# A graph network on one core: the store of the count rows issued by ScalarE instead of by SyncE

## The chip, the cores and the metric

The kernel runs on one core of one Trainium2 chip. The metric is the device time of one execution in microseconds (us), the median of several runs. The engines are TensorE (PE in the profile; PEld is its weight load), VectorE (DVE), ScalarE (ACT), GpSimd (POOL) and SyncE (SP). A row with "SPq" or "ACTq" is a transfer issued by that engine; the time in it is how long the engine stood at the issuing instruction, not how long the data took.

## The reference

The inputs are 6250 nodes of 128 features and 206250 edges, sorted by destination, with a weight each. Four layers are added to x one after the other, each on `h = relu(layernorm(x))`:

```python
x = x + segment_sum(w[:, None] * (sigmoid(h @ Wg + bg) * (h @ W))[dst], src)   # L0
x = x + segment_sum(h[src], dst) @ W1.T + b1                                   # L1
x = x + layer 2: messages from h[src] and h[dst] summed at dst, then a linear update
x = x + layer 3: hypergraph convolution, batch norm over all nodes, relu
```

All four need sums over the same edges. The kernel makes them dense: a matrix of edge counts between nodes, and for L0 the matrix of edge weights.

## The kernel before

The nodes lie in 49 tiles of 128 (`TILES`). After a preparation of about 240 us comes the *build*, one pass over the 49 tiles `j`. It makes for each tile 128 rows of three matrices, each 128 x 6272 numbers in fp16: the counts, and the weights as a high and a low part. It also carries L0 along. Then four phases (`ph` 1 to 4) multiply the stored counts with the node features.

In the build a tile is made in 8 steps `h` of 2 units `u`, 16 units in all:

- VectorE (`hots`, lines 788 to 791) writes one-hot tiles `hot_c` and `hot_r`, two buffers deep. It also adds finished sums to X (`add_four`, line 803), 13 a tile.
- TensorE (`half_windows`, lines 531 to 533) multiplies them into PSUM, 12 matmuls a unit. `take_high` (line 514) subtracts the high part again, so that the low part is left. `sums` (lines 506 to 508) multiplies the turned weights of tile j - 2, `wt`, with the gated features, `g_in`. This is L0, and it waits for both transposing transfers of tile j - 2 before its first product, in step h = 0.
- ScalarE (`build`, line 1033) copies counts and high parts of each unit from PSUM to `stage`, and in `low_parts` (line 1016) the low part two units later. `stage[:, b]` has three slabs (0 counts, 1 high, 2 low) and two buffers, `b` = j mod 2. Before it writes the first unit of tile j, ScalarE waits for what tile j - 2 still needs of the same buffer: `stored{b}` and `wt_in{b}`.
- SyncE (`hand_on`) issues the transfers of a tile. The whole queue is in program order.

The body of `hand_on` before the change, with a = 0 for the high and a = 1 for the low part:

```python
sp.wait_ge(s(done), (j + 1) * HALVES)             # hi_done, then lo_done
sp.dma_start(g_in[:, b, part], ...)               # L333
sp.dma_start_transpose(wt[:, b, a], stage[...])   # L334, slab 1 + a
...
sp.dma_start(by_source...[:, :, cols], stage[:, b, 0])   # L336, the store of the counts
```

So for each tile the queue of SyncE holds: g_in and the transposing transfer of the high part, the same of the low part, and last the store of the counts, 1568 KB into the DRAM matrix `by_source` (counts_by_source in the profile), in runs of 256 bytes. Before them SyncE waits (line 332) until the sums of tile j - 2 are done. After tile 0 a second store (line 339, `filled`) writes a column block of padding.

The stores must have landed before phase 1: `counts_stored` is waited for by SyncE, ScalarE and VectorE. The tiles 0 to 6 are written out one by one, the others run in a loop over six tiles at a time.

Of the kernel before, what the change touches and what calls it, by code (L numbers as in the profile page):

```python
# [19 lines left out]
P = 128  # L20
NODES, EDGES = 6250, 206250
TILES = -(-NODES // P)
# [27 lines left out]
HALVES = 2 * TILE_HOTS  # L50
# [73 lines left out]
def gnn_kernel(nc, x, src, dst, edge_weight, w0, wg0, bg0, w1, b1, wm, bm, wu, bu, hyper, w3, b3, gamma, beta, out):  # L124
    ctx = ExitStack()
    with ctx:
# [159 lines left out]
        @block.sync  # L286
        def _(sp):

            for a, b in ((dst, dst_pad), (src, src_pad), (edge_weight.bitcast(I32), w_pad)):
                sp.dma_start(b[0:EDGES].rearrange("(a b) -> a b", a=15), a.rearrange("(a b) -> a b", a=15)).then_inc(s("pad_in"), 16)  # L290
            sp.wait_ge(s("pads"), 2)
            for k, b in ((1, dst_pad), (0, src_pad), (0, w_pad)):
                sp.dma_start(vec(b[EDGES:PADDED]), pad_rows[0:1, k, :]).then_inc(s("pad_in"), 16)

            sp.dma_start(X[:, 0:TILES - 1, :], x[0:(TILES - 1) * P].rearrange("(i p) f -> p i f", p=P)).then_inc(s("x_in"), 16)
            sp.wait_ge(s("x_zero"), 1)
            sp.dma_start(X[0:LAST, TILES - 1, :], x[(TILES - 1) * P:NODES]).then_inc(s("x_in"), 16)

            for to, of in ((w0g[:, 0:P], w0), (w0g[:, P:P + 1], wg0), (w3s[:], w3), (w_h[:, 0], wu[0:P]),
                           (wraw[:, 0], w1), (wraw[:, 1], wm[0:P]), (wraw[:, 2], wm[P:2 * P]), (wraw[:, 3], wu[P:2 * P]),  # L300
                           (b1s[:], spread(b1, P)), (bus[:], spread(bu, P)), (cols[:, 4:5], spread(bg0, 1)),
                           (cols[:, 0:1], bm.rearrange("(a b) -> a b", b=1)), (cols[:, 1:2], b3.rearrange("(a b) -> a b", b=1)),
                           (cols[:, 2:3], gamma.rearrange("(a b) -> a b", b=1)), (cols[:, 3:4], beta.rearrange("(a b) -> a b", b=1))):
                sp.dma_start(to, of).then_inc(s("weights_in"), 16)
            sp.wait_ge(s("x_zero"), 2)
            sp.dma_start(hrows[0:TILES - 1, :], hyper[0:(TILES - 1) * P].rearrange("(i p) -> i p", p=P)).then_inc(s("weights_in"), 16)
            sp.dma_start(hrows[TILES - 1:TILES, 0:LAST], vec(hyper[(TILES - 1) * P:NODES])).then_inc(s("weights_in"), 16)

            sp.wait_ge(s("pad_in"), 96)
            sp.dma_start(dst_run[:], bass.AP(dst_pad.tensor, 0, [[RUN, P], [1, RUN + 1]])).then_inc(s("dst_in"), 16)  # L310
            sp.dma_start(w_run[:], bass.AP(w_pad.tensor, 0, [[RUN, P], [1, RUN]])).then_inc(s("w_in"), 16)
            for k, b in enumerate((src_pad, dst_pad, w_pad)):
                sp.dma_start(table[:, k * P:(k + 1) * P], bass.AP(b.tensor, 0, [[ALIGN, ROWS], [1, P]])).then_inc(s("table_in"), 16)  # L313

            def layers(general):
                if general:
                    for ph in range(5):
                        general_sum(ph)
                    return

                sp.wait_ge(s("g_parts"), SET)
                sp.dma_start(g_dram.rearrange("i p n -> p i n"), G[:].rearrange("p i a f -> p i (a f)")).then_inc(s("g_stored"), 16)
                sp.wait_ge(s("g_stored"), 16)

                def hand_on(j, k, c):

                    b = c % 2
                    if later(j, 2):
                        sp.wait_ge(s("four_done"), (j - 1) * FOURS)
                    for a, done in enumerate(("hi_done", "lo_done")):  # L330
                        part = slice(a * P, (a + 1) * P)
                        sp.wait_ge(s(done), (j + 1) * HALVES)
                        sp.dma_start(g_in[:, b, part], slab(g_dram, j)[:, part]).then_inc(s(f"g_loaded{b}"), 16)  # L333
                        sp.dma_start_transpose(wt[:, b, a], stage[:, b, 1 + a].rearrange("p i d -> p (i d)")).then_inc(s(f"wt_in{b}"), 16)  # L334
                    cols = slice(j * P, (j + 1) * P) if isinstance(j, int) else bass.ds(j * P, P)
                    sp.dma_start(by_source.rearrange("i p n -> p i n")[:, :, cols], stage[:, b, 0]).then_inc(s(f"stored{b}"), 16)  # L336
                    if isinstance(j, int) and j == 0:

                        sp.dma_start(by_source.rearrange("i p n -> p i n")[:, :, TILES * P:], stage[:, b, 0]).then_inc(s("filled"), 16)

                tiles_loop(sp, hand_on, 0)
                counts_stored(sp)
                sp.wait_ge(s("added"), FOURS * TILES)

                for ph in (1, 2, 3, 4):

                    def step(j, k, c, ph=ph):
                        if not on(j):
                            return
                        if ph == 4:  # L350
                            if later(j, SLOTS):

                                sp.wait_ge(s("sum_done4"), j - (SLOTS - 1))
                            else:
                                sp.wait_ge(s("sum_done3"), min(TILES, 46 + c // 2 * 2))
                            sp.dma_start_transpose(a_turned[:, c % SLOTS], slab(by_source, j)[:, 0:TILES * P]).then_inc(s(f"turned_in{c % SLOTS}"), 16)  # L356
                        elif c % 2 == 0:
                            if later(j, SLOTS):

                                sp.wait_ge(s(f"sum_done{ph}"), j - (SLOTS - 2))  # L360
                            elif ph > 1:
                                sp.wait_ge(s(f"sum_done{ph - 1}"), min(TILES, 46 + c))
                            q = pair_at(ph, c) % 3
                            rows = by_source.rearrange("i p n -> p i n")
                            cols = slice(j * P, (j + 2) * P) if isinstance(j, int) else bass.ds(j * P, 2 * P)
                            sp.dma_start(a_pairs[:, q].rearrange("p i a d -> p i (a d)"), rows[:, :, cols]).then_inc(s(f"a_in{q}"), 16)

                    tiles_loop(sp, step, 0)

            def general_sum(ph):  # L370

                sp.wait_ge(s("g_rows_all"), ph + 1)
                sp.dma_start(h_dram.rearrange("(i p) f -> p i f", p=P), rows_all[:]).then_inc(s("g_table"), 16)
                with sp.Fori(0, CHUNKS) as c:
                    sp.wait_ge(s("g_free"), c + (ph * (CHUNKS + 1) + 1))
                    for a, b in enumerate((src_pad, dst_pad, w_pad)):
                        sp.dma_start(edge_in[:, a:a + 1], b[bass.ds(c * P, P)].rearrange("(a b) -> a b", b=1)).then_inc(s("g_in"), 16)

            branch(sp, layers)

            for g in range(6):
                sp.wait_ge(s("x_out"), 8 * (g + 1))
                sp.dma_start(out[g * 8 * P:(g + 1) * 8 * P].rearrange("(i p) f -> p i f", p=P), X[:, g * 8:(g + 1) * 8, :]).then_inc(s("out_stored"), 16)
            sp.wait_ge(s("x_out"), TILES)
            sp.dma_start(out[(TILES - 1) * P:NODES], X[0:LAST, TILES - 1, :]).then_inc(s("out_stored"), 16)
            sp.wait_ge(s("out_stored"), 16 * 7)
# [595 lines left out]
        def _(act):  # L982
# [29 lines left out]
            def layers(general):  # L1012
# [5 lines left out]
                def build(j, k, c):  # L1018
                    b, n = c % 2, k * (SLOTS // 2) + c // 2
                    for u in range(HALVES):  # L1020
                        if later(j, 1) or u >= 2:
                            act.wait_ge(s("low_left"), j * HALVES + (u - 1))
                            low_parts(*before_at(b, c, u))
                        if u == 0 and later(j, 2):

                            act.wait_ge(s(f"stored{b}"), n * 16)
                            act.wait_ge(s(f"wt_in{b}"), n * 32)
                            if isinstance(j, int) and j == 2:
                                act.wait_ge(s("filled"), 16)
                        act.wait_ge(s("unit_done"), j * HALVES + (u + 1))  # L1030
                        bank = 2 * unit_at(c, u)
                        of = ps[:, bank:bank + 2, 0:HALF * WCOLS].rearrange("p k (i x) -> p k i x", i=TILES)
                        a.copy(stage[:, b, 0:2, :, u * SET_COLS:(u + 1) * SET_COLS], of).then_inc(s("hi_done"), 1)  # L1033

                if not general:
                    act.wait_ge(s("g_stored"), 16)
# [94 lines left out]
```

## Time and profile before

| what | value |
|---|---|
| median of 3 runs | 2862.77 us (2861.38 to 2884.23) |
| the profiled execution | 2846.73 us |
| its span on the core | 2844.9 us, mean granted clock 0.954 |
| first and last transposing transfer of the build issued | 244.9 and 1493.6 us |
| mean moved by DMA, whole span | 212 GB/s |

The span is the time from the first to the last instruction on the core. The profiled execution is one run; the median is of other runs. In the rows below, a row of a timeline gives the start in us, the duration in us, engine, line, operation, and in brackets the idle time before it and what ended that.

### The profile page before, as it was taken

To read this page: it belongs to the slowest core of one execution; us is meant where nothing else is said; L and a number is where in the kernel's file an instruction comes from. 1 tells how busy PE (TensorE), PEld (TensorE's weight loads), DVE (VectorE), ACT (ScalarE), POOL (GpSimd) and SP (SyncE) were. 2 spreads that over 40 slices of the span, in tenths; PEclk is the share of its full clock that TensorE was granted. 3 is DMA by queue.
4 is the path that set the end of the run, shared out by engine and by line. 5 is a ranking of instruction groups with operands and counts; after the bars stand their busy time and mean duration, and the time that the engine had idled before them with its cause. 6 is when DMAs were issued, how large, how long until landed. Compare 5 with 4: busy or idle time off the path is not lost.

```text
span 2844.9 us, 72345 instructions
## 1 busy us (share of the span) xinstructions
PE 2373.2 (83%) x27975; PEld 2024.3 (71%) x27975; DVE 1614.5 (57%) x3456; ACT 1214.5 (43%) x2626; POOL 66.4 (2%) x59
## 2 busy tenths in 40 slices
PE   1626898888888888898893999869997799999996
PEld 0414777777776777777772888758886688888884
DVE  5387998898898988898985111232223222212114
ACT  0605777776776777776773000141112211111113
POOL 0430000000000000000000000000000000000000
PEclk9999999999999999999996999979999899999997
DMA  9615999999999999999997999959999699999995
GB/s 280 181 45 114 195 198 196 193 186 195 188 189 188 196 178 200 181 203 193 183 204 185 264 278 274 280 150 251 258 250 257 167 289 291 283 240 252 252 252 121
DMA packets 1784416, 603.26 MB, mean 212 GB/s; under 512 B 1258086, under 2 KB 1781098, under 8 KB 1784093
## 3 DMA queue, kind: packets, MB, share of 16 engines
q1 hardware_dynamic: 1782538, 594.63, 97.8%
q0 software_dynamic: 1600, 4.92, 0.6%
q8 instruction: 176, 2.88, 0.4%
q14 instruction: 102, 0.84, 0.1%
HBM read 276.78 MB, written 109.03 MB: 136 GB/s over the span
## 4 chain that ended last, share of the span: by engine, by line
PE 43%; SPq 21%; DVE 10%; DMA 9%; issue 9%; ACT 6%; DVEq 1%; POOL 1%; ACTq 0%; POOLq 0%
PE ps L578 30%; SPq L334 10%; SPq L356 9%; DMA counts_by_source<-stage 7%; DVE X L803 4%; PE ps L506 3%; PE ps L508 2%; PE ps L507 2%; ACT hbig L992 2%; DMA edge_table<-w_pad 2%; DVE hot_c L791 2%; ACT stage L1033 2%; ACT stage L1016 1%; PE ps L531 1%; SPq L313 1%
## 5 line engine op out<-in xcount | busy, mean ns | idle before, releaser
L578 PE MATMUL ps<-Ha,a_pairs 128*128 128x258 f16 x7203 | 827.0, 275 | 103.6 <-ACT Ha L1061 103.6
L578 PEld LDWEIGHTS ps<-Ha,a_pairs 128*128 128x128 f16 x7203 | 705.3, 98 | 214.8 <-ACT Ha L1061 104.3
L1033 ACT CAST stage<-ps 128x784 f16<-128x784 f32 x784 | 653.5, 834 | 221.3 <-DMA counts_by_source<-stage 98.8
L531 PE MATMUL ps<-hot_c,hot_r 128*128 128x98 f16 x3136 | 517.1, 214 | 11.6 <-DVE hot_c L791 7.4
L532 PE MATMUL ps<-hot_c,hot_r 128*128 128x98 f16 x3136 | 511.7, 213 | 0.0
L533 PE MATMUL ps<-hot_c,hot_r 128*128 128x98 f16 x3136 | 510.7, 213 | 0.0
L1016 ACT CAST stage<-ps 128x392 f16<-128x392 f32 x784 | 396.5, 506 | 208.0 <-PE ps L514 207.9
L506 PE MATMUL ps<-g_in,wt 128*128 128x128 f16 x2401 | 438.5, 225 | 45.4 <-DVE X L803 32.6
L1072 ACT COPY extra<-ps 128x2 f32 (+1 forms) x196 | 31.4, 160 | 1037.9 <-PE ps L578 1037.9
L507 PE MATMUL ps<-g_in,wt 128*128 128x128 f16 x2401 | 435.0, 224 | 0.0
L508 PE MATMUL ps<-g_in,wt 128*128 128x128 f16 x2401 | 434.0, 223 | 0.0
L803 DVE SCALAR_TENSOR_TENSOR X<-ps,X 128x512 f32<-128x512 f32 (+1 forms) x637 | 394.0, 659 | 16.8 <-PE ps L508 15.6
L791 DVE TENSOR_TENSOR hot_c<-hot_c,meta_w 128x1568 f16<-128x1568 f16 x392 | 382.4, 976 | 0.0
L531 PEld LDWEIGHTS ps<-hot_c,hot_r 128*128 128x128 f16 x3136 | 311.5, 99 | 86.7 <-ACT stage L1016 41.8
L514 PE MATMUL ps<-stage,minus 128*128 128x392 f16 x784 | 265.6, 339 | 125.6 <-ACT stage L1033 72.1
L532 PEld LDWEIGHTS ps<-hot_c,hot_r 128*128 128x128 f16 x3136 | 314.1, 100 | 20.7 <-issue 1.6
L533 PEld LDWEIGHTS ps<-hot_c,hot_r 128*128 128x128 f16 x3136 | 314.0, 100 | 0.0
L506 PEld LDWEIGHTS ps<-g_in,wt 128*128 128x128 f16 x2401 | 240.4, 100 | 84.9 <-DVE X L803 74.0
L788 DVE TENSOR_TENSOR hot_c<-iota_c,meta 128x784 f16<-128x784 f16 x392 | 221.9, 566 | 135.7 <-PE ps L533 109.1
L578 PE MATMUL ps<-Hb,a_turned 128*128 128x258 f16 x2401 | 278.0, 274 | 18.7 <-DMA a_turned<-counts_by_source 15.6
L901 DVE TENSOR_TENSOR agg<-ps,low 128x128 f32<-128x128 f32 x98 | 28.6, 292 | 433.4 <-ACT low L1075 433.4
L578 PEld LDWEIGHTS ps<-Hb,a_turned 128*128 128x128 f16 x2401 | 231.9, 98 | 59.6 <-DMA a_turned<-counts_by_source 15.7
(176 smaller groups left out, 2083.3 us busy)
## 6 DMA issues: line engine op xcount, KB each, us to landing
a_pairs<-counts_by_source SPq DMA_DIRECT2D x75, 3136.0 KB, 14.0
counts_by_source<-stage SPq DMA_DIRECT2D x50, 1568.0 KB, 9.6
edge_table<-src_pad SPq DMA_DIRECT2D x1, 6464.0 KB, 27.9
edge_table<-dst_pad SPq DMA_DIRECT2D x1, 6464.0 KB, 49.5
edge_table<-w_pad SPq DMA_DIRECT2D x1, 6464.0 KB, 48.0
gated_parts<-G SPq DMA_DIRECT2D x1, 3136.0 KB, 12.6
g_in<-gated_parts SPq DMA_DIRECT2D x98, 32.0 KB, 3.3
out_x<-X SPq DMA_DIRECT2D x6, 512.0 KB
```

Of the source, the lines that this page charges most:

```text
L334: sp.dma_start_transpose(wt[:, b, a], stage[:, b, 1 + a].rearrange("p i d -> p (i d)")).then_inc(s(f"wt_in{b}"), 16)
L506: mm(o, wt[:, b, 0, i], g_in[:, b, 0:P], start=i % 4 == 0, stop=False, skip_group_check=True)
L507: mm(o, wt[:, b, 0, i], g_in[:, b, P:2 * P], start=False, stop=False, skip_group_check=True)
L508: last = mm(o, wt[:, b, 1, i], g_in[:, b, 0:P], start=False, stop=True, skip_group_check=True)
L531: mm(into(0), rows_, codes(0), start=v == 0, stop=True, skip_group_check=True)
L532: mm(into(1), rows_, codes(1), start=v == 0, stop=False, skip_group_check=True)
L533: last = mm(into(1), rows_, codes(2), start=False, stop=True, skip_group_check=True)
L578: last = mm(ps[:, c % 2, 0:PARTS], a_slot(ph, c, i), moving[:, i], start=i == 0, stop=i == TILES - 1)
L791: v.tensor_tensor(hot_c[:, b, :, 1:1 + WEIGHTS], hot_c[:, b, :, 0].unsqueeze(2).to_broadcast([P, PAIRS, WEIGHTS, WCOLS, 2]), meta_w[:, pai ...
L803: v.scalar_tensor_tensor(xs, ps[:, 6 + e, 0:(hi - lo) * P], 1.0 / (W_UP * H_UP), xs, ALU.mult, ALU.add).then_inc(s("added"), 1)
L1016: a.copy(stage[:, b, 2, :, u * SET_COLS:(u + 1) * SET_COLS], of).then_inc(s("lo_done"), 1)
L1033: a.copy(stage[:, b, 0:2, :, u * SET_COLS:(u + 1) * SET_COLS], of).then_inc(s("hi_done"), 1)
```

## The change

The store of the counts and the padding store leave SyncE's queue. ScalarE issues them after the copy of the last unit of tile j, once all 16 copies of that tile are complete. Semaphores, sources, destinations and sizes are the same. The lines behind the removed ones move up by 5; line 1033 (the copy of counts and high parts) is line 1028 in the changed kernel, and line 1016 (the low part) is line 1011.

```diff
@@ hand_on, SyncE @@
                         sp.dma_start_transpose(wt[:, b, a], stage[:, b, 1 + a].rearrange("p i d -> p (i d)")).then_inc(s(f"wt_in{b}"), 16)
-                    cols = slice(j * P, (j + 1) * P) if isinstance(j, int) else bass.ds(j * P, P)
-                    sp.dma_start(by_source.rearrange("i p n -> p i n")[:, :, cols], stage[:, b, 0]).then_inc(s(f"stored{b}"), 16)
-                    if isinstance(j, int) and j == 0:
-
-                        sp.dma_start(by_source.rearrange("i p n -> p i n")[:, :, TILES * P:], stage[:, b, 0]).then_inc(s("filled"), 16)
@@ build, ScalarE @@
                         a.copy(stage[:, b, 0:2, :, u * SET_COLS:(u + 1) * SET_COLS], of).then_inc(s("hi_done"), 1)
+                    store_counts(j, b)
+
+                def store_counts(j, b):
+
+                    act.wait_ge(s("hi_done"), (j + 1) * HALVES)
+                    cols = slice(j * P, (j + 1) * P) if isinstance(j, int) else bass.ds(j * P, P)
+                    a.dma_start(by_source.rearrange("i p n -> p i n")[:, :, cols], stage[:, b, 0]).then_inc(s(f"stored{b}"), 16)
+                    if isinstance(j, int) and j == 0:
+
+                        a.dma_start(by_source.rearrange("i p n -> p i n")[:, :, TILES * P:], stage[:, b, 0]).then_inc(s("filled"), 16)
```

On SyncE, the written-out tiles 0 and 1 of the build, before (L336 and L339 are the two kinds of store):

```order
L333 DMA g_in<-gated_parts 128x128
L334 DMA_TRANSPOSE wt<-stage 128x49x128
L333 DMA g_in<-gated_parts 128x128
L334 DMA_TRANSPOSE wt<-stage 128x49x128
L336 DMA counts_by_source<-stage 128x49x128
L339 DMA counts_by_source<-stage 128x49x128
L333 DMA g_in<-gated_parts 128x128
L334 DMA_TRANSPOSE wt<-stage 128x49x128
L333 DMA g_in<-gated_parts 128x128
L334 DMA_TRANSPOSE wt<-stage 128x49x128
L336 DMA counts_by_source<-stage 128x49x128
```

and the same two tiles now:

```order
L333 DMA g_in<-gated_parts 128x128
L334 DMA_TRANSPOSE wt<-stage 128x49x128
L333 DMA g_in<-gated_parts 128x128
L334 DMA_TRANSPOSE wt<-stage 128x49x128
L333 DMA g_in<-gated_parts 128x128
L334 DMA_TRANSPOSE wt<-stage 128x49x128
L333 DMA g_in<-gated_parts 128x128
L334 DMA_TRANSPOSE wt<-stage 128x49x128
```

Only the two pairs of a tile are left on SyncE; nothing stands between the second transposing transfer of a tile and the first g_in of the next.

On ScalarE, the border between tile 0 and tile 1, before (the copies of counts and high parts and of low parts alternate without a break):

```order
L1016 CAST stage<-ps 128x49x8
L1033 CAST stage<-ps 128x98x8
L1016 CAST stage<-ps 128x49x8
L1033 CAST stage<-ps 128x98x8
L1016 CAST stage<-ps 128x49x8
```

and now:

```order
L1011 CAST stage<-ps 128x49x8
L1028 CAST stage<-ps 128x98x8
L1035 DMA counts_by_source<-stage 128x49x128
L1038 DMA counts_by_source<-stage 128x49x128
L1011 CAST stage<-ps 128x49x8
L1028 CAST stage<-ps 128x98x8
```

The store stands behind the last copy of counts and high parts of its tile (L1028), and ahead of the low parts (L1011) of that tile's last two units. The padding store comes in tile 0 only.

## Rows read from the trace of the kernel before

**Rows 1.** The page: busy engines, the SP queue, the largest transfers
```profile
PE 2373.2 (83%) x27975; PEld 2024.3 (71%) x27975; DVE 1614.5 (57%) x3456; ACT 1214.5 (43%) x2626; POOL 66.4 (2%) x59
...
DMA  9615999999999999999997999959999699999995
...
q1 hardware_dynamic: 1782538, 594.63, 97.8%
```

**Rows 2.** Waits: engine, line waited for; us in total, times, longest
```profile
ACT stage L1033 <- DMA counts_by_source<-stage: 98.8, 23, 15.7
...
PEld ps L506 <- DMA wt<-stage: 9.9, 2, 8.6
```

**Rows 3.** Timeline of SyncE's queue, two tiles of the build
```profile
351.47 0.33 SPq L333 DMA_DIRECT2D g_in<-gated_parts  x1
351.84 8.71 SPq L334 DMA_TRANSPOSE wt<-stage  x1
360.60 0.58 SPq L333 DMA_DIRECT2D g_in<-gated_parts  x1
361.22 7.64 SPq L334 DMA_TRANSPOSE wt<-stage  x1
368.91 0.58 SPq L336 DMA_DIRECT2D counts_by_source<-stage  x1
374.56 1.78 SPq L333 DMA_DIRECT2D g_in<-gated_parts  x1
...
401.81 0.33 SPq L333 DMA_DIRECT2D g_in<-gated_parts  x1
```

**Rows 4.** Timeline of ScalarE at a border of two tiles
```profile
374.30 0.57 ACT L1016 CAST stage<-ps 128x392 f16<-128x392 f32 x1
378.28 0.81 ACT L1033 CAST stage<-ps 128x784 f16<-128x784 f32 x1 [3.41 <-DMA counts_by_source<-stage]
378.99 0.49 ACT L1016 CAST stage<-ps 128x392 f16<-128x392 f32 x1
```

**Rows 5.** Timeline of VectorE, the same border
```profile
381.67 0.57 DVE L788 TENSOR_TENSOR hot_c<-iota_c,meta 128x784 f16<-128x784 f16 x1 [2.61 <-PE ps L533]
```

**Rows 6.** Timeline of SyncE's queue: first g_in of tile 2 and of the last tile
```profile
300.64 0.33 SPq L333 DMA_DIRECT2D g_in<-gated_parts  x1
...
1484.45 0.35 SPq L333 DMA_DIRECT2D g_in<-gated_parts  x1
```

**Rows 7.** The page, transfers: issues, KB each, median us from issue to landing
```profile
counts_by_source<-stage SPq DMA_DIRECT2D x50, 1568.0 KB, 9.6
...
wt<-stage SPq DMA_TRANSPOSE x98, 11.0
```

**Rows 8.** Lines 334 and 336: ns at the issuing instruction, min/median/max
```profile
L334 SPq DMA_TRANSPOSE wt<-stage x98: 7337/7922/8987, 244.9 to 1493.6; - x98
...
L336 SPq DMA_DIRECT2D counts_by_source<-stage x49: 439/447/1097, 261.1 to 1501.2; - x49
```

**Rows 9.** Timeline of SyncE's queue, the two stores after tile 0
```profile
261.14 0.59 SPq L336 DMA_DIRECT2D counts_by_source<-stage  x1
261.77 7.16 SPq L339 DMA_DIRECT2D counts_by_source<-stage  x1
268.97 7.33 SPq L333 DMA_DIRECT2D g_in<-gated_parts  x1
```

**Rows 10.** Stretches: us, busy, granted clock (1.00 is full), DMA share, GB/s
```profile
316.00:318.00 2.00, 1.84 (x34) 1.56 (x32) 2.00 (x4) 1.93 (x4) 0.00 (x0) 1.00 1.17 217
320.00:322.00 2.00, 1.79 (x26) 1.10 (x23) 2.00 (x5) 2.00 (x5) 0.00 (x0) 1.00 1.04 218
...
300.00:1480.00 1180.00, 1032.07 (x16289) 892.52 (x16288) 1063.92 (x1697) 865.81 (x1466) 0.00 (x0) 0.96 1.08 192
```

**Rows 11.** Timeline of TensorE in the sums: two matmuls in a row
```profile
1484.57 0.22 PE L507 MATMUL ps<-g_in,wt 128*128 128x128 f16 x1
...
1484.63 0.22 PE L508 MATMUL ps<-g_in,wt 128*128 128x128 f16 x1
```

## Prediction

> **What bounds the kernel now.** I read the page first, for who is busy, then the waits, for who stops whom, and then the timelines of SyncE, ScalarE and VectorE over two tiles of the build. The page shows TensorE busiest over the whole span and the DMA engines at nine tenths almost everywhere [rows 1]. Nearly all of it goes through SyncE's one queue. The waits name the store directly: ScalarE stands at line 1033 for 98.8 us in 23 waits until a store has landed. The turned weights are hardly ever waited for by TensorE: 9.9 us in two waits [rows 2]. So at first sight the store is late and should go earlier.
>
> The timeline of SyncE shows the rhythm. Its first g_in of a tile marks the tile's end, because it waits for the last copy. The ends are at 351.5, 374.6 and 401.8 us: one tile of 23.1 us and one of 27.2 us [rows 3]. The short one is a tile in which nobody waits. The long one contains the wait: ScalarE's last copy ends at 374.9 us, and it goes on at 378.28, when the store of the tile before has landed [rows 4]. The wait of 3.41 us reaches VectorE as 2.61 us [rows 5]; the other 0.8 us is slack in its buffers. From the end of tile 2 to the end of the last tile, 46 tiles take 1484.45 - 300.64 = 1183.8 us, 25.73 a tile [rows 6]. Against 23.1 that is 2.63 us a tile, 121 us in all. That is the most that the change can bring in the build. I use a pair of tiles, one short and one long, as the unit; there are 24 pairs.
>
> What sets the long tile is the time from the end of a tile to the landing of its last transfer: 378.28 - 351.47 = 26.8 us, against 23.1 us that the next tile gives it [rows 3, 4]. It is made of 0.4 us to the first transposing transfer, 8.7, 0.6 and 7.6 us up to the end of the second, and 9.4 us for the store.
>
> **The change part by part.** *Taken off SyncE.* 49 stores and one padding store, with a median of 0.447 us at the instruction [rows 8]. That is a saving of some 0.4 us in a trio (two transposing transfers and a store), for the issue is done beside SyncE's. -0.4 us a pair.
>
> *The store's own time.* Here is the main point. While a store is being worked off, SyncE cannot push the next transfer: the padding store stands 7.16 us behind the first store, and the g_in behind it another 7.33 us [rows 9]. In the loop the store was issued at 368.91, and the g_in of 374.56 was held until 376.3, again 7.4 us after it [rows 3]. A transposing transfer holds SyncE for 7.34 us at least and 7.92 us in the middle [rows 8]. Both are 1568 KB (128 x 6272 numbers of two bytes), and both move 217 to 218 GB/s in a stretch of their own [rows 10]: 1.606 MB at 217 GB/s is 7.4 us. So one limit of the DMA engines holds for both, and three transfers need 3 x 7.4 = 22.2 us whatever their order. ScalarE waits for all three of them before it reuses the buffer. Putting the store first makes it land early and both transposing transfers later. I take the gain from order alone as 0.
>
> *The gaps.* Over the build the mean is 192 GB/s of those 217 [rows 10]. The transposing transfers take 2 x (7.9 - 7.4) = 1.0 us more than the limit, and the g_in between them 0.6 twice. A store on another queue could fill these. Bounds: 0, if the second queue is held as SyncE's own next transfer is in rows 9, and -2.2 us a pair. I take -0.4, near the held rows, which are the only ones with two large transfers.
>
> A rule of the Trainium skill stands beside this one. In "DMA: Bandwidth & Descriptors", section "Issuing engines are not separate DMA queues", it says that transfers started by different engines run on the same 16 DMA engines, and that issuing from several only saves the issue time. The shared limit of 217 GB/s agrees with it [rows 10]. By the rule alone the sum would be the first term only, about -10 us.
>
> *What is last now.* The last of the trio becomes the second transposing transfer. It lands 11.0 us after issue, so 3.1 us after SyncE is free of it (11.0 - 7.9); the store lands 9.6 us after issue, 2.2 us after its 7.4 [rows 7, 8]. +0.9 us a pair.
>
> *A wait that takes the place.* TensorE used to do the first sums of tile j - 2 while ScalarE stood: two groups of four, 24 matmuls at 0.06 us, 1.4 us (two in a row start at 1484.57 and 1484.63) [rows 11]. They need both transposing transfers. If these land when ScalarE is released, the sums are done after the wait instead of in it, ahead of the next unit. Bounds 0 and +1.4 us a pair; ScalarE's two copies at 0.7 us [rows 4] run beside it, so I take +0.4.
>
> *Added on ScalarE.* The wait for its own copy and the issue, about 0.1 + 0.45 us a tile [rows 8]. Behind them are queued the low parts of the last two units, and TensorE waits for those. In the long tile the store wait follows and hides this; in the short one it meets the 0.8 us of slack above. 0 if hidden. If the issue is held like the g_in in rows 3, it is 1.8 us. I take +0.1 a pair. The padding store after tile 0 will hold ScalarE some 7 us, but it has a wait of 15.7 us there already [rows 2], which shrinks by as much.
>
> *The end of the build.* After the last tile nothing follows to hide behind. TensorE waits 8.6 us for the last weights [rows 2]. With the store ahead of or among them they land up to 7.4 us later. Bounds 0 and +7.4, I take the middle, +3.7.
>
> The sum: (-0.4 - 0.4 + 0.9 + 0.4 + 0.1) = +0.6 us a pair, times 24 is +14.4; with the end +18.1 us. On the profiled execution, 2846.7 becomes 2864.8 us. The runs shown have a median 16 us above it, so against 2862.8 I forecast 2881 us, +0.6%.
>
> **The rivals.** *Faster: the two queues really run beside each other.* For it speaks the gap between 192 and 217 GB/s. With the gaps filled the trio takes 0.4 + 22.2 + 3.1 = 25.7 us instead of 26.8: -1.1 x 24 = -26 us, 2837. If two queues also lift the 217 itself, the trio fits into 23.1 us and the whole 121 us go: 2742. Against it: rows 9 show one large transfer at a time, and the size of the work does not change.
>
> *Slower: the transposing transfers pay for the store.* Place: the store, issued at the tile's end, takes turns with the first transposing transfer, piece by piece, and each turn costs. A time of 3 us more in the trio gives 24 x 3 = 72 us, with the terms above 2950; at 1.2 us more it is 2910. It decides from the point at which the second one lands more than 27.5 us after the tile's end, because then TensorE and ScalarE both stand. Against it: no row shows turns that cost.
>
> The Trainium skill describes such turns in "DMA: Bandwidth & Descriptors", section "Queues, rings and completion order": each DMA engine goes round the queues that have work, a packet at a time. No row here shows it, as there is only one busy queue; by it alone both would be slow together and the sum is unchanged.
>
> *Slower: ScalarE is held at its issue.* If SyncE's pushes keep it standing for 1.8 us or more, the short tiles lose 1.0 us or more after the slack, 24 us and up: 2905.
>
> *The store was not late at all.* That the change does nothing would need the wait to be on something else; the timeline has the wait's end at the landing, so I give it no weight.
>
> **How the numbers follow.** About 1% is what a measurement of this kernel can tell from no change. The forecast (work conserved, wait moved to the transposing transfers) gets 0.45, of which 0.30 within 1% and 0.15 above. The faster rival gets 0.27: 0.22 beyond 1%, 0.05 within. The turns get 0.18, nearly all slower. ScalarE held gets 0.10, half within. Together: faster 0.22, within 1% 0.40, slower 0.38. The range runs from 2800, well into the faster rival, to 2930, into the turns; outside are some 0.1 on each side. The forecast's own range is 2860 to 2900.
>
> **What would show it right or wrong.** In the changed profile the wait of ScalarE at its first copy (line 1028) should be put down to the transfer wt<-stage instead of the store, with about the same total. TensorE's wait for wt at line 501 (506 before) should grow from 2 waits to some 20. The store should land well before the transposing transfers of its tile. SyncE should stand up to 7.4 us longer in the first g_in or the first transposing transfer of each tile. Pairs should take 51 to 52 us, short tiles still 23.1 us. I am wrong if pairs take under 50 us and DMA runs above 200 GB/s over the build (then the queues run side by side), or if the store's landing takes over 15 us and the pairs over 53 us (then turns cost).

## The result and the profile after

| | median | range | runs |
|---|---|---|---|
| before | 2870.14 us | 2861.38 to 2884.23 | 4 |
| changed | 2912.23 us | 2911.40 to 2912.51 | 4 |

The ratio is 1.0141, 95% interval 1.0112 to 1.0169: the change makes the kernel 1.4% slower; the medians are 42 us apart. The forecast was 2881 us, with a range from 2800 to 2930.

The page of the changed kernel, against [rows 1]: the same bytes, with the stores on a queue of their own (q10).

```profile
span 2909.6 us, 72387 instructions
...
PE 2375.8 (82%) x27975; PEld 2027.8 (70%) x27975; DVE 1620.6 (56%) x3456; ACT 1219.1 (42%) x2626; POOL 66.3 (2%) x59
...
DMA  9613999999999999999999899969999699999995
...
q1 hardware_dynamic: 1468138, 514.34, 83.4%
q10 hardware_dynamic: 314400, 80.28, 14.9%
```

The waits, against [rows 2] (engine, line waited for; us in total, times, longest). Lines are 5 lower than before. "issue" is idle time in which the engine waits for nothing that the profile shows.

```profile
DVE X L798 <- PE ps L503: 68.1, 41, 10.8
...
ACT stage L1028 <- DMA wt<-stage: 65.4, 22, 8.9
PE ps L501 <- DMA wt<-stage: 65.1, 20, 9.6
...
ACT stage L1011 <- issue: 29.5, 6, 9.2
```

No wait for a store is left. The wait of ScalarE is now for the transposed weights, and TensorE has one for them too, 65.1 us in 20 where it had 9.6. VectorE waits for the sums that TensorE makes late (68.1 us, 15.6 before). The last row is new: ScalarE stands 9.2 us behind the padding store, and 3.4 to 4.7 us in five of the six tiles behind the loop's jump. The kernel before has no such row for a copy.

SyncE's queue over two tiles, against [rows 3]:

```profile
344.18 7.31 SPq L334 DMA_TRANSPOSE wt<-stage  x1
351.59 0.53 SPq L333 DMA_DIRECT2D g_in<-gated_parts  x1
352.16 15.72 SPq L334 DMA_TRANSPOSE wt<-stage  x1
367.93 0.58 SPq L333 DMA_DIRECT2D g_in<-gated_parts  x1
368.55 7.72 SPq L334 DMA_TRANSPOSE wt<-stage  x1
376.37 1.26 SPq L333 DMA_DIRECT2D g_in<-gated_parts  x1
377.68 13.86 SPq L334 DMA_TRANSPOSE wt<-stage  x1
```

ScalarE's queue and its first copies in the same stretch, against [rows 4]:

```profile
351.51 0.39 ACTq L1035 DMA_DIRECT2D counts_by_source<-stage  x1
...
353.64 0.81 ACT L1028 CAST stage<-ps 128x784 f16<-128x784 f32 x1 [1.22 <-DMA wt<-stage]
...
375.42 0.38 ACTq L1035 DMA_DIRECT2D counts_by_source<-stage  x1
...
380.86 0.81 ACT L1028 CAST stage<-ps 128x784 f16<-128x784 f32 x1 [4.54 <-DMA wt<-stage]
```

The first transposing transfer of a tile holds SyncE for 15.7 us instead of 8.7: it shares the engines with the store. The second takes 7.7 us as before. But the store of the *next* tile is issued at 375.42, before SyncE is through with the second at 376.27, and ScalarE is released only at 380.86. From the tile's end to the release that is 380.86 - 351.51 = 29.4 us. A tile earlier the store was issued at 351.51, just when SyncE was through (344.18 + 7.31 = 351.49), and ScalarE was released 2.1 us later, at 353.64.

Is this one step typical? From tile 2 on, ScalarE's first copy of a tile was released by the transfer wt<-stage 21 times. In 10 of them the next tile's store had been issued more than 0.4 us before SyncE was through with the second transposing transfer, and the release came 3.2 to 5.1 us after SyncE was through. In the other 11 it came 2.0 to 3.1 us after it. The step above is of the long kind, and the 26.8 us of the prediction belong to one of the shortest chains of the kernel before. From the end of a tile's last copy to the release, over all waits that a transfer ended, the median was 28.3 us before (21 waits, 26.1 to 29.4) and is 27.5 us now (21 waits): 27.9 to 30.1 in the 10, 25.3 to 27.5 in the 11. So the typical chain of three transfers did not grow; its long form did.

Issues and landing, against [rows 7, 8] (us to landing in the first, ns at the instruction in the second):

```profile
counts_by_source<-stage ACTq DMA_DIRECT2D x50, 1568.0 KB, 13.9
```

```profile
L334 SPq DMA_TRANSPOSE wt<-stage x98: 7311/13206/16636, 267.1 to 1557.3; - x98
```

The mean rate of the same stretch of the build, against [rows 10], fell from 192 to 187 GB/s:

```profile
300.00:1480.00 1180.00, 1006.24 (x15817) 871.27 (x15818) 1035.04 (x1644) 845.78 (x1425) 0.00 (x0) 0.95 1.10 187
```

Where the time went, by the timelines of SyncE. The first g_in of tiles 0, 2 and 48, and the first transfer of phase 1:

```profile
266.72 0.34 SPq L333 DMA_DIRECT2D g_in<-gated_parts  x1
...
327.99 0.34 SPq L333 DMA_DIRECT2D g_in<-gated_parts  x1
...
1540.94 1.47 SPq L333 DMA_DIRECT2D g_in<-gated_parts  x1
...
1578.55 9.88 SPq L361 DMA_DIRECT2D a_pairs<-counts_by_source  x2
```

The two spans differ by 2909.6 - 2844.9 = 64.7 us. It splits into the preparation up to tile 0 (266.7 against 244.5, +22.2), tiles 0 and 1 (+5.1), tiles 2 to 48 (1212.95 against 1183.81, +29.1), the end of the build (37.6 against 31.05, +6.6), and the rest, +1.7. The first is no effect of the change. In the runs below the build starts at 265.6 to 267.5 us in four kernels that ran on one chip, and at 243.6 to 246.3 us in the eight that ran on another or others, whichever queue the stores were on. So the two profiles most likely came from different chips, though their record does not name the chip. Before, the build started at 244.5 us and phase 1 at 1515.5 us. Without the first part 42.5 us are left, which fits the 42 us between the medians.

### The profile page after: what moved, and what is told of

Same layout as the page of the kernel before. It is cut to its first block, busy times and chain, and to the rows that moved or that the text cites. A ratio compares the mean times of both kernels' runs of the same rounds, so it can differ in the third digit from the quotient of the medians.

```text
span 2909.6 us, 72387 instructions
## 1 busy us (share of the span) xinstructions
PE 2375.8 (82%) x27975; PEld 2027.8 (70%) x27975; DVE 1620.6 (56%) x3456; ACT 1219.1 (42%) x2626; POOL 66.3 (2%) x59
## 4 chain that ended last, share of the span: by engine, by line
PE 44%; SPq 19%; DVE 11%; issue 9%; DMA 8%; ACT 7%; DVEq 1%; another core or an unknown queue 1%; ACTq 1%
PE ps L573 29%; SPq L334 9%; SPq L351 9%; DMA wt<-stage 8%; DVE X L798 4%; PE ps L501 3%; PE ps L503 2%; PE ps L502 2%; ACT hbig L987 2%; ACT stage L1028 2%; ACT stage L1011 2%; DVE hot_c L786 1%; PE ps L526 1%; PE ps L528 1%; PE ps L527 1%
## 5 line engine op out<-in xcount | busy, mean ns | idle before, releaser
L1028 ACT CAST stage<-ps 128x784 f16<-128x784 f32 x784 | 652.4, 832 | 190.0 <-PE ps L528 103.4
L501 PE MATMUL ps<-g_in,wt 128*128 128x128 f16 x2401 | 441.8, 226 | 102.2 <-DMA wt<-stage 65.1
L1011 ACT CAST stage<-ps 128x392 f16<-128x392 f32 x784 | 391.3, 499 | 267.6 <-PE ps L509 238.1
L798 DVE SCALAR_TENSOR_TENSOR X<-ps,X 128x512 f32<-128x512 f32 (+1 forms) x637 | 394.7, 657 | 68.4 <-PE ps L503 68.1
L527 PEld LDWEIGHTS ps<-hot_c,hot_r 128*128 128x128 f16 x3136 | 313.8, 100 | 24.2 <-issue 5.1
L509 PE MATMUL ps<-stage,minus 128*128 128x392 f16 x784 | 266.7, 340 | 54.2 <-DVE hot_c L786 28.4
L784 DVE TENSOR_TENSOR hot_r<-iota_r,meta 128x1024 f16<-128x1024 f16 x392 | 270.2, 689 | 0.0
## 6 DMA issues: line engine op xcount, KB each, us to landing
counts_by_source<-stage ACTq DMA_DIRECT2D x50, 1568.0 KB, 13.9
```

Of the source, the lines that this page charges most:

```text
L501: mm(o, wt[:, b, 0, i], g_in[:, b, 0:P], start=i % 4 == 0, stop=False, skip_group_check=True)
L527: mm(into(1), rows_, codes(1), start=v == 0, stop=False, skip_group_check=True)
L784: v.tensor_tensor(hot_r[:, b], iota_r[:].unsqueeze(1).to_broadcast([P, PAIRS, P, 2]), key(0, P), ALU.is_equal)
L798: v.scalar_tensor_tensor(xs, ps[:, 6 + e, 0:(hi - lo) * P], 1.0 / (W_UP * H_UP), xs, ALU.mult, ALU.add).then_inc(s("added"), 1)
L1011: a.copy(stage[:, b, 2, :, u * SET_COLS:(u + 1) * SET_COLS], of).then_inc(s("lo_done"), 1)
```

## The experiments

"A tile" is the mean of the 46 spacings between the first instruction of tile 2 and of tile 48 in SyncE's queue. A "plain" tile is any other than the jump tiles; the "jump" tiles are the six behind the loop's jump back (the first of each round of six). Ratios are to the kernel before, run on the same chip. Two ratios can also be compared across the groups, but only to some 0.3%, the half-width of their intervals. The chips differ: the median of the kernel before was 2871.6, 2845.2 and 2851.2 us in the three groups, so ratios are compared and not times.

| kernel | median us | ratio (95%) | a tile | plain | jump |
|---|---|---|---|---|---|
| before | | 1 | 25.73 | 23.1, every other up to 28.8 | 27.9 to 31.2 |
| changed | 2912.2 | 1.0141 (1.0112 to 1.0169) | 26.37 | 23.4 to 28.8 | 31.2 to 33.3 |
| sp_first | 2854.3 | 0.9945 (0.9928 to 0.9963) | 25.26 | 23.4 to 26.9 | 28.3 to 29.5 |
| sp_first_act_tiny | 2829.3 | 0.9942 (0.9917 to 0.9967) | 25.21 | 23.7 to 26.9 | 29.3 to 29.9 |
| sp_last_three | 2760.7 | 0.9618 (0.9597 to 0.9639) | 23.78 | 23.1 | 27.8 to 29.3 |
| act_three | 2840.6 | 0.9890 (0.9868 to 0.9912) | 25.24 | 23.9 | 34.0 to 35.1 |
| act_late_three | 2777.4 | 0.9674 (0.9653 to 0.9695) | 23.89 | 23.1 | 28.7 to 30.0 |
| before_aligned | 2747.1 | 0.9646 (0.9611 to 0.9680) | 23.83 | 23.1 | 27.9 to 29.9 |
| after_aligned | 2817.0 | 0.9891 (0.9856 to 0.9927) | 25.25 | 23.9 | 34.0 to 34.9 |
| three_unaligned | 2784.9 | 0.9781 (0.9746 to 0.9815) | 24.45 | 23.1 to 25.7 | 27.8 to 28.6 |
| before_aligned_act_tiny | 2801.9 | 0.9838 (0.9811 to 0.9865) | 24.86 | 23.7 | 32.0 to 33.5 |
| after_aligned_u4 | 2772.7 | 0.9733 (0.9707 to 0.9760) | 24.10 | 23.1 | 28.9 to 31.7 |
| sp_first_aligned | 2768.8 | 0.9726 (0.9696 to 0.9756) | 24.05 | 23.1 | 27.8 to 30.9 |
| after_sums_shift | 2923.6 | 1.0255 (1.0217 to 1.0292) | 27.29 | 24.2 to 29.4 | 34.0 to 36.2 |

**The order alone, in one queue (sp_first).**

```diff
                     if later(j, 2):
                         sp.wait_ge(s("four_done"), (j - 1) * FOURS)
+                    sp.wait_ge(s("hi_done"), (j + 1) * HALVES)
+                    cols = ...
+                    sp.dma_start(by_source...[:, :, cols], stage[:, b, 0]).then_inc(s(f"stored{b}"), 16)
                     for a, done in enumerate(("hi_done", "lo_done")):
...
-                    sp.dma_start(by_source...[:, :, cols], stage[:, b, 0]).then_inc(s(f"stored{b}"), 16)
```

> The store stays on SyncE's queue but goes ahead of the two transposing transfers instead of behind them. Theory of order (what counts is that the transposing transfers land last, about 27 us after the tile's end, and that TensorE and ScalarE both wait for them): 26.2 to 26.6 us a tile between tile 2 and the last, TensorE waits for wt in 15 to 25 tiles, time within 0.4% of the changed kernel (2900 to 2925 us). Rival, turns (the loss comes from two queues taking turns packet by packet, and from the issue on ScalarE): neither is there, so the time is that of the kernel before (2860 to 2880 us).

Measured: 0.9945, faster than before. Neither theory foresaw a gain. The loss is not in the order; against this kernel the change is 2.0% behind (1.0141/0.9945). Nor is it in the waits for wt as such, for this faster kernel has them too, and larger than the changed one:

```profile
ACT stage L1034 <- DMA wt<-stage: 79.8, 28, 14.8
...
PE ps L507 <- DMA wt<-stage: 72.4, 26, 13.9
```

Its queue:

```profile
520.63 0.41 SPq L332 DMA_DIRECT2D counts_by_source<-stage  x1
521.22 6.53 SPq L339 DMA_DIRECT2D g_in<-gated_parts  x1
527.80 8.82 SPq L340 DMA_TRANSPOSE wt<-stage  x1
536.81 0.45 SPq L339 DMA_DIRECT2D g_in<-gated_parts  x1
537.30 7.58 SPq L340 DMA_TRANSPOSE wt<-stage  x1
545.21 0.41 SPq L332 DMA_DIRECT2D counts_by_source<-stage  x1
```

The g_in is held for 6.5 us behind the store, as the forecast had it for one queue. From 521.22 to the end of the first transposing transfer it is 15.4 us, as long as the 15.7 us in which store and transfer ran side by side. So running them together saved nothing. What differs is the end. Here are the last copy of a tile and two releases of ScalarE:

```profile
518.86 0.89 ACT L1034 CAST stage<-ps 128x784 f16<-128x784 f32 x1
...
522.99 0.81 ACT L1034 CAST stage<-ps 128x784 f16<-128x784 f32 x1 [2.85 <-DMA wt<-stage]
546.63 0.81 ACT L1034 CAST stage<-ps 128x784 f16<-128x784 f32 x1 [1.37 <-DMA wt<-stage]
```

The second transposing transfer had been pushed by 544.88 and released ScalarE 1.8 us later; over the 27 such steps from tile 2 on it took 1.4 to 3.8 us. In the changed kernel it took 380.86 - 376.27 = 4.6 us where the next tile's store came in 0.85 us before the end of the push, and 2.1 us where it did not. Here the store of a tile is mostly issued late, because SyncE is still busy: the tile ended at 518.86 + 0.89 = 519.75, the store came at 520.63. From the tile's end to the release it is 546.63 - 519.75 = 26.9 us, which is also the median of the 27. In one queue the next store was behind that push in all 27; from its own queue it comes in ahead of the push's end.

**The stand of ScalarE at the border (sp_first_act_tiny).** The same order, and at each tile's end:

```diff
+                    act.wait_ge(s("hi_done"), (j + 1) * HALVES)
+                    a.dma_start(tiny[j], minus16[0:1, :]).then_inc(s("tiny"), 16)   # 256 bytes; index shortened
```

> The store first on SyncE's queue, as in the run of that order, and besides ScalarE waits for its last copy and issues a transfer of 256 bytes at the end of each tile, where the change issues the store. Theory (the loss of the change is the stand of ScalarE at the border of two tiles, where it is full): 0.6 to 1.1 us a tile more than the same kernel without the small transfer, 2885 to 2910 us. Rival (the loss is that the store and the first transposing transfer take turns on the DMA engines): the small transfer costs under 0.2 us a tile, 2854 to 2865 us.

Measured: 0.9942 against 0.9945, nothing. In this kernel the stand is covered by other waits. But does that hold for the changed kernel too? Here are the tiles 3 to 48 by the end of ScalarE's last copy, which no queue delays (short is under 24.3 us; us):

| kernel | short tiles, median | long tiles, mean | six jump tiles, mean |
|---|---|---|---|
| before | 23 of 23.1 | 17 of 27.6 | 30.3 |
| sp_first | 24 of 23.1 | 16 of 26.2 | 30.3 |
| sp_first_act_tiny | 26 of 23.7 | 14 of 25.7 | 30.3 |
| changed | 26 of 23.9 | 14 of 28.1 | 32.6 |

With the small transfer the short tiles grow by 0.6 us and the long ones shrink by as much in all (1160 us for the 46 tiles without it, 1159 with it): that is the cover. In the changed kernel the short tiles grow by 0.8 us, the long ones do not shrink, and the jump tiles grow by 2.3 us each. These last are 14 of the 51 us by which its 46 tiles are longer than those of sp_first, and in five of the six ScalarE stands, some 7 us after the store's issue. A row from the first of them:

```profile
593.14 0.49 ACT L1011 CAST stage<-ps 128x392 f16<-128x392 f32 x1 [3.83 <-issue]
```

So the 2.0% belong to the store issued by ScalarE on its own queue. The overtaking can be one part of them and ScalarE's stand, in the short tiles and behind the jump, another; no run takes them apart. That would be the changed kernel, not aligned, with its store issued a microsecond later or a few units into the next tile.

**Three buffers for the counts.** The counts get slabs 0 to 2 of `stage`, by j mod 3; high and low parts keep two.

```diff
-        stage, o = at("stage", [P, 2, 1 + WEIGHTS, TILES, P], F16, o)
+        stage, o = at("stage", [P, 3 + 2 * WEIGHTS, TILES, P], F16, o)
...
-                            act.wait_ge(s(f"stored{b}"), n * 16)
+                            if later(j, 3):
+                                act.wait_ge(s(f"stored{c % 3}"), (k * 2 + c // 3) * 16)
...
-                        a.copy(stage[:, b, 0:2, :, u * SET_COLS:(u + 1) * SET_COLS], of)
+                        a.copy(stage[:, c % 3:4 + b:3 + b - c % 3, :, u * SET_COLS:(u + 1) * SET_COLS], of)
```

With the store last on SyncE (sp_last_three):

> The kernel before (store last, on SyncE) with three buffers for the counts slab, so that ScalarE waits for the store of tile j - 3 instead of j - 2; the high and low slabs keep two. Theory (the long tile is the buffer's wait for the last transfer of the trio, not the DMA's work as such): ScalarE's waits for the store vanish, a tile takes 23.5 to 24.6 us, time 2790 to 2830 us. Rival, work (the DMA engines are full as they are, and any freed wait comes back as a wait for wt): 25.3 us a tile or more, within 1% of before.

With the store issued by ScalarE at the tile's end (act_three):

> The changed kernel (store on ScalarE's queue) with the same three buffers for the counts. Theory (the wait has moved to the transposing transfers): the third buffer frees nothing, 26.0 to 26.6 us a tile, within 0.5% of the changed kernel (2898 to 2925 us). Rival (the store is still what ScalarE waits for): it gains as much as the same buffers do with the store on SyncE, 60 us or more.

And issued by ScalarE ten units later (act_late_three):

> Three buffers for the counts, store on ScalarE's queue but issued ten units later, in the middle of the next tile, when the transposing transfers of its tile are nearly through. Theory (what costs is that the store is ahead of or among the transposing transfers, not which engine issues it): as the three buffers with the store last on SyncE, 23.5 to 24.6 us a tile, 2790 to 2830 us. Rival (the issue on ScalarE or the second queue costs by itself): 20 us or more slower than that one.

Measured: 0.9618, 0.9890 and 0.9674. The first and the last were even faster than the theory had it (2790 to 2830 us), the second seemed to refute it, for it gained 2.5% on the changed kernel where nothing was expected. But in all three SyncE stood 6.2 to 6.9 us (medians) in the second transposing transfer of a tile, instead of 7.9. One small tile had been moved and an unused one dropped to make room, and `stage` and `wt` had come to begin at a multiple of 256 bytes. Two causes were in one run, so I took them apart.

**The address alone.** Line 187, in the kernel before and in the changed one; `stage` began 192 bytes past a multiple of 256:

```diff
+        o += 64
         stage, o = at("stage", [P, 2, 1 + WEIGHTS, TILES, P], F16, o)
```

> The kernel before, with the tiles stage and wt moved up by 64 bytes, so that both begin at a multiple of 256 bytes (they began 192 bytes past one); in the runs with three buffers they happened to. Theory (the address of the 256-byte runs sets the time of a transposing transfer): SyncE stands 6.2 to 7.0 us at each instead of 7.9, the long tile shrinks by 2 us or more, time 2800 to 2830 us. Rival (the shorter transfers of the runs with three buffers come from less waiting, not from the address): 7.9 us and the time of before.

> The changed kernel with the same 64 bytes. Theory (the move costs ScalarE's time at the border whatever the transfers take): the address gains as much as in the kernel before or a little less, and the changed kernel stays 20 to 50 us behind it. Rival (the move costs only because the trio was too long for a tile): with shorter transfers the two are level within 10 us.

Measured: 0.9646 for the one (2747 us, better than the expected 2800 to 2830) and 0.9891 for the other (70 us behind it, more than the expected 20 to 50). SyncE's time in a transposing transfer of the aligned kernel before (ns, min/median/max), against [rows 8]:

```profile
L335 SPq DMA_TRANSPOSE wt<-stage x98: 5932/6732/8276, 245.3 to 1398.9; - x98
```

It is 6.7 us instead of 7.9, the store lands after 8.6 us instead of 9.6 [rows 7], and with that the long tile is gone: plain tiles of 23.1 us throughout. 64 bytes give 3.5%, more than the change costs. The changed kernel stays behind by 2.5% (0.9891/0.9646), more than without the 64 bytes.

And the same three buffers with the old address (192 bytes more):

> Three buffers for the counts, store last on SyncE, but stage and wt again 192 bytes past a multiple of 256. Theory (buffer and address are two separate gains, and the buffer takes ScalarE's wait away even with the slow transfers, up to the DMA's 23.2 us of a trio): 23.5 to 24.6 us a tile, 2775 to 2815 us. Rival (all of the gain was the address): level with before, 2860 us or more.

Measured: 0.9781. Buffer and address are separate gains, of 2.2% and 3.5%, and together 3.8%: each takes away much of the same wait (ScalarE's waits for transfers were 98.8 us; 45.1 are left with the buffer alone, 11.9 with the address alone). And act_three (0.9890) is level with after_aligned (0.9891): in the aligned kernel the third buffer frees nothing once the store is on ScalarE's queue. This is a weak test of the theory, since in after_aligned ScalarE waits for a transfer only once, for 0.7 us.

**What the move costs where nobody waits.** In the aligned pair, plain tiles are 23.1 and 23.9 us. Plain tiles of before_aligned:

```profile
578.32 0.34 SPq L334 DMA_DIRECT2D g_in<-gated_parts  x1
...
601.44 0.33 SPq L334 DMA_DIRECT2D g_in<-gated_parts  x1
```

and of after_aligned:

```profile
613.35 0.34 SPq L334 DMA_DIRECT2D g_in<-gated_parts  x1
...
637.26 0.34 SPq L334 DMA_DIRECT2D g_in<-gated_parts  x1
```

ScalarE at the border of after_aligned: the last copy of a tile, the issue, the next low part.

```profile
612.30 0.89 ACT L1029 CAST stage<-ps 128x784 f16<-128x784 f32 x1
613.34 0.43 ACTq L1036 DMA_DIRECT2D counts_by_source<-stage  x1
613.88 0.48 ACT L1012 CAST stage<-ps 128x392 f16<-128x392 f32 x1 [0.70 <-PE ps L510]
```

In before_aligned a copy starts each 0.71 us after the one ahead without a break there (623.50, then 624.21). Here the low part starts 1.58 us after the copy: 0.87 us of stand, where ScalarE's copies otherwise follow one another without idle time. I tested whether this is the cost.

```diff
+                    act.wait_ge(s("hi_done"), (j + 1) * HALVES)
+                    a.dma_start(tiny[j], minus16[0:1, :]).then_inc(s("tiny"), 16)   # before_aligned_act_tiny
```

> The aligned kernel with the store last on SyncE, and ScalarE issues a transfer of 256 bytes at the end of each tile, behind the wait for its last copy. In the aligned pair nobody waits for a transfer in most tiles, so a stand is not covered. Theory (the 0.8 us that the move adds to a plain tile is ScalarE's stand at the border): 23.9 us for a plain tile, and 28.6 us for the tile behind the loop's jump, 30 to 40 us over the aligned kernel before (0.977 to 0.98 of before). Rival (it is the store taking turns with the transposing transfer): plain tiles stay at 23.1 us, level with the aligned kernel before (0.965).

```diff
-                    store_counts(j, b)
+                        if u == 4 and later(j, 1):        # after_aligned_u4
+                            store_counts(j - 1, 1 - b)
...
+                    store_counts(TILES - 1, 0)            # behind the last tile
```

> The aligned changed kernel with the store issued on ScalarE four units into the next tile (about 5 us after the border), two buffers as before; the store still runs beside the transposing transfers. Theory (the border is what costs): plain tiles 23.1 us, the tile behind the jump 31 us or less, 50 to 70 us faster than the aligned changed kernel (0.965 to 0.972 of before). Rival (turns on the DMA engines cost): plain tiles 23.6 us or more, within 15 us of the aligned changed kernel (0.985 to 0.990).

Measured: with the small transfer 0.9838, plain tiles 23.7 us and jump tiles 32.0 to 33.5; with the store some 5 us past the border 0.9733, 45 us better than after_aligned where 50 to 70 were expected, plain tiles 23.1 us again and jump tiles 28.9 to 31.7. The stand makes 1.03 of the 1.42 us a tile that the move costs in the aligned pair (24.86 and 25.25, less 23.83). The jump tiles were not foreseen in the first of the two: they grew by some 4 us, which is about half of the 1.03. Its waits for "issue" have a row of ScalarE:

```profile
ACT stage L1036 <- issue: 31.7, 6, 5.8
```

and those of after_aligned:

```profile
ACT stage L1012 <- issue: 55.1, 9, 7.9
```

The kernel aligned before has no such row. As in the changed kernel, ScalarE now stands behind the jump, with nothing that the profile shows to wait for. What it stands for no row names.

**The order alone, aligned.**

> Aligned, store first on SyncE's queue. Theory (order alone costs nothing once the trio fits into a tile): 23.1 us for plain tiles, level with the aligned kernel before within 12 us (0.961 to 0.969 of before), plus some 6 us at the end, where the last weights land later. Rival (late weights hold TensorE in the first step of a tile even so): 0.4 us a tile or more on top, 0.972 or more.

Measured: 0.9726, 0.8% (23 us) behind before_aligned and outside the 12 us; the ratio is where the rival had it, but not for its reason. Plain tiles are 23.1 us as expected; the jump tiles are longer (up to 30.9), and the end of the build takes 32.6 us from the last tile (1402.35 to 1434.93) instead of 27.7 (1391.8 to 1419.49).

**TensorE's sums one step later.**

```diff
-                        if later(j, 2):
-                            sums(j - 2, c % 2, k * (SLOTS // 2) + c // 2, h)
+                        if later(j, 2) and h:
+                            sums(j - 2, c % 2, k * (SLOTS // 2) + c // 2, h - 1)
```

> The changed kernel (not aligned) with the sums of tile j - 2 one step later in TensorE's order, so that it makes two more units before it needs the transposed weights. Theory (TensorE's new wait for wt, 65 us in 20 tiles, is a part of the loss): that wait falls under 25 us and the time by 10 to 30 us, to 1.004 to 1.011 of before. Rival (ScalarE waits for the same transfers at the same moment, so TensorE's wait costs nothing of its own): within 6 us of the changed kernel (1.012 to 1.016).

Measured: 1.0255, slower than the changed kernel, against both theories. Its waits, the first of which was 68.1 us in the changed kernel:

```profile
DVE X L798 <- PE ps L503: 182.9, 74, 11.2
```

TensorE's wait for wt did go (14.3 us in 2). But VectorE adds a sum two steps after TensorE's place for it, and with the shift only one step is left between them, so VectorE waited longer instead. So this run does not price TensorE's wait. What it is worth stays open; sp_first, with 72.4 us of it, says only that it is not what sets the changed kernel 2.0% apart.

## Why the prediction was right, and where a step failed

The direction and the range from 2800 to 2930 held. The size was under half: +18 us forecast, 42 measured, and the forecast's own range of 2860 to 2900 was missed. That the wide range held is owed to the room that it kept for the rivals. By steps:

- *The wait moves to the transposing transfers.* Right in kind. ScalarE's wait for the store (98.8 us in 23) is 0, and for wt there are 65.4 us in 22, less than the "about the same total" of the forecast. TensorE waits for wt in 20 tiles, as said. But sp_first has both waits and is faster than before, so they do not explain the loss.
- *The store's own time, taken as 0.* Right for the work: side by side or one after the other, store and first transposing transfer took 15.7 and 15.4 us. Wrong for the order: store first in one queue gave 0.5 us a tile (25.73 to 25.26). From the tile's end to the release the median is then 26.9 us, not 28.3.
- *The gaps, -0.4.* Wrong. Nothing was filled: from the tile's end to the end of the second transposing push the median is 24.4 us over the waits above, and 24.0 with one queue. The 187 GB/s are the same bytes in a longer time.
- *What is last now, +0.9.* Mis-sized, and not evenly. The forecast took the landing of the second transposing transfer from runs in which nothing could overtake it. The next tile's store does: 3.2 to 5.1 us from push to release in the 10 waits with it, 2.0 to 3.1 in the 11 without, 1.4 to 3.8 in one queue. That the overtaking is the cause is read from the timelines; what the runs show is that one queue in the same order loses none of the 2.0%.
- *ScalarE's stand, +0.1.* This is the other term that was mis-sized. The forecast had it hidden, short tiles "still 23.1 us" and nothing at the jump. Measured are 23.9 us in 26 short tiles and 2.3 us more in each of the six jump tiles, 14 us, half of the 27 us by which tiles 3 to 48, by their last copies, are longer than before. The cover that the forecast counted on was seen in sp_first_act_tiny (0.9942 against 0.9945), but not in the changed kernel. In the aligned kernel the stand is 1.03 us a tile.
- *The start, 0, and the end, +3.7.* Measured +5.1 and +6.6; the end is near its bound of 7.4.
- *The sum.* +0.6 us a pair was forecast. Measured are 29.1 us over 23 pairs, 1.3 us a pair: pairs of 52.7 us, where 51 to 52 were forecast.

Of the rivals, "the transposing transfers pay for the store" was nearest. It put the limit at 27.5 us from a tile's end, and up to 30.1 were seen. Its reason (each turn costs) is not seen: store and first transposing transfer took as long side by side as one after the other. Its two signs, pairs over 53 us and a landing of the store over 15 us, were not reached (52.7 and 13.9). "The two queues really run beside each other" is refuted by the 15.7 us. "ScalarE is held at its issue" is wrong for the issue itself (0.38 to 0.49 us), but near the truth behind the jump, where ScalarE now stands 3.4 to 4.7 us at one copy. What sets the limit of 217 GB/s was taken as fixed and was not: 64 bytes of address moved it.

## What to carry to other kernels

Here a second queue made no room on DMA engines that were full; it took away the order. A transfer that nobody needs soon can then run ahead of one that an engine waits for, so put urgent and patient transfers in one queue, urgent ones as early as possible, or give the patient one a buffer more. When an issue must go to a compute engine, put it where that engine has idle time in each step, not at the border where it has none, and look at the iterations behind a loop's jump by themselves: that is where much of this loss was. Read a chain's length from many steps and not from one. And when an experiment needs room, look where its buffers come to lie before believing its gain.

## What was not expected of the hardware

- Moving the source and destination of a transposing transfer from 192 bytes past a multiple of 256 onto one cut SyncE's time in it from 7.9 to 6.7 us, and the whole kernel by 3.5%. The Trainium skill has a reason in "DMA: Bandwidth & Descriptors", section "How a descriptor splits into AXI transactions": a read has to start at a multiple of 256 bytes, so a run that does not is fetched in more pieces. The runs agree in direction: the packets of both kinds of transfer are of 256 bytes here (4694 packets for 1.20 MB in a stretch of a transposing transfer).
- Issued from one queue, a plain transfer behind a large one holds its engine until that one is worked off (7.2 and 7.3 us, [rows 9]); issued from another queue it goes at once (0.38 us) and shares the rate.
- In the kernels whose plain tiles take 23.1 us, the tile behind the loop's jump takes 4.6 us or more longer; with the store on ScalarE's queue at the border it is up to 11.2 us longer (act_three, 35.1 against 23.9).

The fastest median ratio is that of three buffers with the store last on SyncE, 0.9618. The kernel before with 64 bytes more, 0.9646, is level with it within the intervals and changes one line.
